# Routed attention that fetches its rows by position, another chunk order ahead of a scan, and 75 idle matmuls in place of 50

## The reference

```
h      = layernorm(x)                       # 8 x 256 x 128
logits = h @ [w_qr; w_kvr].T                # 4 query routes, 4 key routes, per token
for each route g and batch b:
    the 128 tokens with the highest query logit give queries
    the 64 tokens with the highest key logit give keys and values
    keys, values from h[those 64 tokens]; the values are scaled by sigmoid(key logit)
    8 heads of width 64, one learned null key and value in each
    out[g] = attention @ w_out, scaled by sigmoid(query logit), back to its tokens
x += mean of out over the routes that chose a token, or null_token where none did
```

## Time and profile before

| | before |
|---|---|
| median of 3 runs | 3162.34 us (3149.78 to 3163.03) |
| the profiled execution, its own time | 3159.7 us |
| its span | 3158.0 us |
| granted TensorE clock, mean | 0.952 |
| PE busy | 2790.3 us (88%) |
| PEld / DVE / ACT / POOL busy | 1829.7 / 1952.1 / 1404.1 / 1036.9 us |

### The profile page before, as it was taken

The page is one execution under the profiler, slowest core; times in us unless marked ns, Lnnn a source line. Parts: engine busy times, 40 slices in busy tenths (PEclk is TensorE's granted clock), DMA queues, the critical chain, the costliest instruction groups (busy, mean ns, idle before and its releaser), DMA issues. The chain is left out here.

```text
span 3158.0 us, 62333 instructions
## 1 busy us (share of the span) xinstructions
PE 2790.3 (88%) x24321; PEld 1829.7 (58%) x24352; DVE 1952.1 (62%) x4335; ACT 1404.1 (44%) x2960; POOL 1036.9 (33%) x1448
## 2 busy tenths in 40 slices
PE   6999799988799968887888799997999989799997
PEld 2343477756577756565556567764666556456664
DVE  7989555556555576634773566665667646466664
ACT  5655144434244435322553354443555534355553
POOL 4878223223223222312112333330222246212222
PEclk9899799999899989879999899999999999999999
DMA  2000100011000001100101000002222201112221
GB/s 79 1 1 1 54 2 1 2 25 28 1 1 2 1 1 48 66 27 20 29 22 31 15 1 1 1 4 72 67 70 70 70 18 32 59 42 73 81 67 46
DMA packets 54256, 97.07 MB, mean 31 GB/s; under 512 B 6042, under 2 KB 40870, under 8 KB 53200
## 3 DMA queue, kind: packets, MB, share of 16 engines
q1 hardware_dynamic: 52688, 92.49, 9.4%
q0 software_dynamic: 1280, 0.60, 0.1%
HBM read 71.76 MB, written 21.76 MB: 30 GB/s over the span
## 5 line engine op out<-in xcount | busy, mean ns | idle before, releaser
L566 ACT ACTIVATE s_sT<-s_R 128x1024 f32<-128x1024 f32 (+2 forms) x448 | 400.3, 946 | 199.5 <-PE s_R L500 198.6
L601 DVE TENSOR_REDUCE s_negm<-s_R 128x4 f32<-128x1024 f32 x320 | 377.2, 1221 | 153.6 <-PE s_R L471 153.5
L471 PE MATMUL s_R<-s_qk 32*128 32x256 f32 (+2 forms) x3584 | 241.8, 383 | 58.0 <-ACT s_sT L566 33.1
L500 PE MATMUL s_R<-s_qA,s_qk 32*128 32x256 f32 (+2 forms) x3584 | 240.7, 382 | 18.3 <-DVE s_negm L601 11.7
L573 ACT ACTIVATE s_oc<-s_OB 128x256 f32<-128x256 f32 x224 | 85.8, 383 | 338.3 <-PE s_OB L519 338.3
L519 PE MATMUL s_OB<-s_sT,s_v 128*32 128x256 f32 (+2 forms) x3584 | 224.1, 368 | 9.9 <-ACT s_sT L566 6.4
L471 PEld LDWEIGHTS s_R<-s_qk 32*128 32x128 f32 x3584 | 153.9, 185 | 106.1 <-issue 79.6
L616 DVE TENSOR_TENSOR s_qA<-s_qk,s_X 128x256 f32<-128x256 f32 x224 | 94.4, 421 | 194.7 <-PE s_X L531 194.7
L500 PEld LDWEIGHTS s_R<-s_qA,s_qk 32*128 32x128 f32 x3584 | 162.4, 184 | 79.2 <-issue 65.1
L1511 POOL TENSOR_TENSOR s_pr<-s_pr,s_rinv 128x1024 f32<-128x1024 f32 x64 | 121.1, 1893 | 219.6 <-DVE s_rinv L1621 219.6
L1593 ACT ACTIVATE s_pr<-s_S,s_negmax 128x256 f32<-128x256 f32 x256 | 118.5, 470 | 135.5 <-DVE s_negmax L1624 135.5
(11 more groups left out here) (585 smaller groups left out, 6307.9 us busy)
## 6 DMA issues: line engine op xcount, KB each, us to landing
s_wB<-enc_b SPq DMA_DIRECT2D x32, 962.5 KB, 4.8
s_scratch<-s_pk SPq DMA_DIRECT2D x58, 256.0 KB, 2.0
s_qk<-s_scratch SPq DMA_DIRECT2D x232, 64.0 KB
s_wA<-enc_a SPq DMA_DIRECT2D x32, 193.0 KB, 5.0
big<-moe SPq DMA_DIRECT2D x2, 2347.0 KB, 11.0
big<-routed SPq DMA_DIRECT2D x2, 2084.0 KB
all_W<-weights SPq DMA_DIRECT2D x1, 2182.0 KB, 15.5
all_W<-weights SPq DMA_DIRECT2D x1, 2181.5 KB, 10.7
```

Source lines behind the costliest of these rows:

```text
L471: last = pe.matmul(S[h][:, t * T:t * T + hi - lo], b.qk[rows, r % 2, 0, c, t * P:(t + 1) * P], b.qk[rows, r % 2, 1, c, lo:hi], start=(t == ...
L500: last = pe.matmul(b.R[:, a.turned_at(u, h // 2), :][:, h % 2, a.at(kt)], b.qk[rows, r % 2, 1, c, kt * P:(kt + 1) * P], b.qA[rows, u % 2, ...
L566: act.activation(b.sT[:, u % (a.lag + 1), 2 * p:2 * p + 2, 0:a.width], b.R[:, a.turned_at(u, p), 0:a.width], ACT.Exp).then_inc(s.expd, 1)
L601: ins = dve.tensor_reduce(b.negm[:, u % 2, :, at].rearrange("p t h -> p h t"), S.rearrange("p h (t k) -> p h t k", t=TT), AX_X, ALU.max, n ...
```

## The change

**Scan preparation.** ScalarE does `deltas(1)` and `rows(2)` ahead of `gates(3)`, and `deltas(2)` between `exp(0)` and `exp(1)`; TensorE's order follows; VectorE corrects each chunk right after its `add_one`. `keep_busy` goes from 50 matmuls to 75.

**Route stage.** SyncE also writes h to DRAM (`sent`, 1 MB). Each of the 16 rounds gets a `max_index`, which gives the positions of the eight maxima. The running count, the slots and the key mask are gone. The positions, the highest logits and the key logits are turned to have ranks on partitions (`place`, `sig`, `index`), and the count of choices comes from two matmuls on the mask.

**Main stage.** No one-hots for the gather. GpSimd fetches the rows by position with indirect DMAs, two for a unit (`fetch`: 128 rows for queries, 64 for keys), 8 units ahead. TensorE's gather is two transposes for a unit. The key scale goes into ScalarE's copy of v. The scatter's one-hot is made in its turned form at once by VectorE (`place_rows`), after the subtraction of its own unit and ahead of its sum.

```
                     rows(1)
-                    gates(3)
                     deltas(1)
                     rows(2)
+                    gates(3)
                     deltas(2)
...
-                    keep_busy(pe, g, XZ[:, 0, :], 50)
+                    keep_busy(pe, g, XZ[:, 0, :], 75)
...
                     magnitude(0)
                     magnitude(1)
+                    add_one(0)
+                    correct(0)
                     magnitude(2)
...
+                        d.done(dve.max(best[:, eight], work[:, k % 2, :]))
+                        d.mark(dve.match_replace(out=work[:, 1 - k % 2, :], in_to_replace=best[:, eight],
+                                                 in_values=work[:, k % 2, :], imm_value=NEG))
+                        d.done(dve.max_index(found[:, eight], best[:, eight], work[:, k % 2, :]))
...
+                                u = group * NB + bb
+                                at, ring = (bb % 2) * (NQ + NK), u % (2 * NB)
+                                pe.wait_ge(got_q[ring], 16 * (u // (2 * NB) + 1))
+                                pe.transpose(f[:, at:at + NQ], hq[:, ring, :], g.ident[:])
+                                pe.wait_ge(got_k[ring], 16 * (u // (2 * NB) + 1))
+                                last = pe.transpose(f[:, at + NQ:at + NQ + NK], hk[:, ring, :],
+                                                    g.ident[0:NK, 0:NK])
...
-                            for h in range(TT):
-                                pe.transpose(f[:, h * P:(h + 1) * P], sq[:, j % (2 * NB), h, :], g.ident[:])
-                            last = pe.transpose(f[0:H, 2 * P:3 * P], pn[:, j % 2, :], g.ident[:])
+                            last = pe.transpose(f[0:H, 0:P], pn[:, j % 2, :], g.ident[:])
...
+                    def fetch(u):
+                        ring = u % (2 * NB)
+                        q, k = columns(u)
+                        if u >= 2 * NB:
+                            before = u - 2 * NB
+                            pool.wait_ge(f_mm, plan.number[("gather", before // NB, before % NB // 2)] + 1)
+                        pool.indirect_dma_start(hq[:, ring, :], None, sent,
+                                                bass.IndirectOffsetOnAxis(index[:, q:q + 1], 0),
+                                                bounds_check=NTOK - 1, oob_is_err=False).then_inc(got_q[ring], 16)
...
+                    for u in range(NB):
+                        fetch(u)
+                    null_keys(0)
+                    for u in range(NB, 2 * NB):
+                        fetch(u)
...
+                        if i + 2 * NB < U:
+                            fetch(i + 2 * NB)
...
+                    def place_rows(u):
+
+                        c = columns(u)[0]
+                        if u >= 4:
+                            dve.wait_ge(scattered, u - 3)
+                        dve.tensor_scalar(sqT[:, u % 4, :], g.iota_free[:], place[:, c:c + 1], sig[:, 0, c:c + 1],
+                                          ALU.is_equal, ALU.mult).then_inc(placed, 1)
...
                                               ALU.subtract).then_inc(shifted, 1)
-                            if i % NB == 0 and i // NB + 1 < plan.GROUPS:
-                                make_onehots(i // NB + 1)
+                            place_rows(i)
                             dve.wait_ge(expd, i + 1)
```

More of the change, by code:

```diff
@@ L2650, in _ @@
                     activate(3)
+                    deltas(1)
+                    rows(2)
                     gates(3)
-                    deltas(1)
                     exp(0)
-                    rows(2)
+                    deltas(2)
                     exp(1)
-                    deltas(2)
                     rows(3)
@@ L2949, in routed_attention_stage @@
     with Stage(nc, name) as st:
-        sig = st.sb("sig", [P, TT, B, 2 * G])
-        slot = st.sb("slot", [P, TT, B, 2 * G])
+        sig = st.sb("sig", [P, 2, ROWS])
+        place = st.sb("place", [P, ROWS])
+        index = st.sb("index", [P, ROWS], mybir.dt.uint32)
+        sent = nc.dram_tensor(f"{name}_sent", (NTOK, D), F32).ap()
         rcount = st.sb("rcount", [P, TT, B])
@@ L3062, in _ @@
-                    d.done(dve.tensor_tensor(mask[:], work[:], row[:], ALU.not_equal))
-                    d.done(dve.tensor_tensor(mask_kv[:], mask_kv[:], mask[:], ALU.subtract))
-                    d.done(dve.scalar_tensor_tensor(out=mask[:], in0=mask_kv[:], scalar=g.w("r_iskv"), in1=mask[:],
-                                                    op0=ALU.mult, op1=ALU.add))
-                    d.done(dve.tensor_tensor_scan(out=csum[:], data0=ones_row[:], data1=mask[:], initial=0.0,
-                                                  op0=ALU.mult, op1=ALU.add))
@@ L3069, in _ @@
-                    d.done(dve.tensor_tensor(csum[:], csum[:], mask[:], ALU.mult))
-                    dve.tensor_scalar(csum[:], csum[:], -1.0, None, ALU.add).then_inc(slots_ready, 1)
-                    dve.wait_ge(back, 1)
-                    d.done(dve.tensor_copy(slot[:].rearrange("p h b j -> p (h b j)"), ST[:, 0:TT * ROWS]))
-                    d.done(dve.tensor_scalar(chosen[:], slot[:, :, :, 0:G], 0.0, None, ALU.is_ge))
-                    d.done(dve.tensor_reduce(count[:], chosen[:], AX_X, ALU.add))
+                        eight = slice(8 * k, 8 * k + 8)
@@ new lines, in _ @@
+                    dve.tensor_tensor(mask[:], work[:, 0, :], row[:], ALU.not_equal).then_inc(mask_ready, 1)
+                    dve.wait_ge(sig_ready, 1)
+                    d.done(dve.tensor_copy(place[:], ST[:, 0:ROWS]))
+                    d.mark(dve.tensor_tensor(index[:], place[:], g.w("r_first"), ALU.add))
+                    dve.wait_ge(counted, 1)
+                    of = LT[:, 0:TT * B].rearrange("p (h b) -> p h b", h=TT)
+                    d.done(dve.tensor_copy(count[:], of))
@@ L3268, in _, with null_keys @@
                 def _(pool):
-                    def scale_onehots(group):
+                    def null_keys(group):
                         s = plan.unit(group * NB)[0]
@@ L3507, in build_program @@
             if n == min({1, 3} & set(layers), default=None):
-                load = ("routed", P)
+                load = ("routed", T)
             if n == (8 if 8 in layers else min({9, 11} & set(layers), default=None)):
```

140 lines of the change are left out of this document (67 added, 73 removed).

## The result

The change makes the kernel slower: 3183.89 us, median of 5 runs (3183.64 to 3188.6), against 3162.34 for the kernel before. The ratio is 1.0081, with a 95% interval of 1.006 to 1.0101. The forecast was 3157.5, with a range of 3140 to 3175, and the time lies above it. The profiled execution has a span of 3181.9 us, 23.9 more than before.

The account below looks back on a forecast made before the run. TensorE was taken to bound the routed main stages' steady part. Two layers at -0.2 (main -4.6, route +4.4) and the scan's -4.3 gave -4.7: 3155 on the profiled execution, 3157.5 as median, range 3140 to 3175.

Parts of the forecast that it names:

- The new wait: Main stage: `place_rows` waits for the scatter four units back, so iterations with short front work last 6.65 us, not 5.70.
- The rival in which TensorE stays the bound: Main stage: VectorE's wait for the scatter is passed in time; a group takes 28.17, the kernel 3126 us; chance 0.15.
- the sum of the layer: One layer's main stage (-4.6) and route stage (+4.4) together: -0.2 us, twice -0.4.
- I take 1.0: Main stage: the new gather's eight transposes, at 0.11 to 0.13 each, cost TensorE 1.0 us.
- the start: Main stage: waiting for the first fetches costs 5.3 us and a slow clock about 2, together +7.3, bounds +5 and +11.
- The first group: Main stage, first four units: without the one-hots S(2) comes 7.1 after S(0), a gain of 5.4 us.
- The end of the stage: Main stage: iterations 28 to 31 lose 0.95 us each, +3.8, and iteration 32 loses +2.6.
- The route stage: `max_index` adds 0.42 us a round, 16 rounds +6.7; removed work and a shorter tail leave +4.4 a layer.
- The scan preparation: Before the scan: shorter VectorE waits give -2.9 us and a better kept clock 1.4, together -4.3.
- the rival: Scan preparation gains nothing: the wait only moves from chunk 2 to chunk 0 and the clock falls; 3162 us, chance 0.12.
- one wait of about 3.3: Scan preparation: VectorE waits once, 3.3 us from the end of magnitude(1) to the first `add_one`, in place of 6.2.
- the rival on the slow side: Main stage: VectorE and GpSimd hinder each other, each fetch call costs 2.6 us, not 1.3; 3178 us, chance 0.1.

Follow-up runs that it names:

- Run 5: The changed kernel with five buffers for the turned one-hot (`sqT`) in place of four; ratio to the kernel before 0.9996.
- run 4: The changed kernel with only the first eight units' rows fetched and reused, 16 calls a stage in place of 64; 3185.21 us in one run.
- run 12: The changed kernel with five buffers, drains, reordered transposes, 100 scan constants, and constants at main-stage starts and in the first group's gaps; 3121.12 us, ratio 0.9921.
- run 1: The kernel before with 16 more semaphores declared in each routed main stage and never used; 3160.84 us in one run beside 3155.22.
- run 7: The kernel before with only the scan preparation's part of the change: new chunk order and 75 constant matmuls in place of 50; ratio 1.0002.
- run 6: The changed kernel with 30 constant matmuls in place of 5 at each main stage's start and 20 more between the first two gathers; ratio 1.0066.
- run 3: The changed kernel with one drain instruction on GpSimd in each group of four units; ratio to the kernel before 1.0065.

## Why the prediction was wrong

The forecast for the profile was 4.7 us faster, and it is 23.9 slower, 28.6 apart. The two main stages make 17.1 of this (8.8 of it in their first groups, 4.8 in the steady parts, 2.7 at the starts, 0.8 at the ends), the two gaps behind them 9.8, the scan 2.7. The new wait, the main mechanism, was in the sum at nearly its true size. The steps that failed are a cost at the stage's end that had no term, the clock in the first group, and the price of the gather's transposes.

**The new wait was right.** `place_rows` was said to wait for the scatter and to start 0.2 after the next scores: 0.11. The iteration was put at 6.65 and is 6.60, TensorE's idle time at 1.2 and is 1.10, and GpSimd is named as the releaser. Run 5 shows that nothing else holds these iterations above TensorE's own 5.43. The rival in which TensorE stays the bound did not occur; its sum has a slip, since +7.3 - 5.4 - 21.5 - 1.6 is -21.2 and not -20.2, 2 us in its time.

**A step was missing: the gap behind the stage.** The prediction says "In steady state the fetches cost nothing", which run 4 confirms, and the sum of the layer has no term for what is settled afterwards. GpSimd's 64 calls leave 4.7 to 5.1 us a layer to the barrier, about 0.08 each, 9.8 in all. The layers of experts in the trace before gave no hint. The first issues 20 such calls, its stage ends at 1480.92 and the next begins at 1481.92. GpSimd's last call there is over at 1473.60, so that what it leaves (1.6 us by the same price, an estimate) may be settled beside VectorE's last seven microseconds; in s1a GpSimd works to 643.09, 0.6 before the end. This reading was not tested.

**The gather was too cheap.** "I take 1.0" for eight transposes; they take 1.85. The price of 0.13 was that of two like transposes in a row. With 7.27 for the gather in place of 6.65 a group is 30.18, not 29.6, and from S(4) to S(28) six groups gain 10.5 in place of 12.9. (6 x 1.57 is 9.4; the iteration behind S(4) still takes 5.42, because `place_rows` of unit 3, on which its turn depends, has no wait.)

**The start and the first group.** In s1a the start costs 9.4, not 7.3: the queries begin 13.6 us into the stage, not 12.4, and the slow clock costs 2.9 at them alone, where 2 was taken. In s3a it costs 7.9. The first group was to gain 5.4 and gains 1.3 and 0.7. In s1a S(2) comes 8.8 after S(0), not 7.1, and the iteration with the queries takes 9.34 where it takes 6.92 at full clock (run 12). The step that failed is the one that took the slow clock to be over once the front had run: it fell again at 400, after the idle gaps of the first softmax. Run 12, with these gaps filled, has the first group at 21.4, 4.6 less than before the change. The kernel before has a slow clock in its first group too (mean 0.87), and that group took 26.0 in its profile and 24.4 in run 1, so a forecast of it is no better than 1.6 us. The end of the stage was right in s1a, 6.1 against 6.4; in s3a it was 7.5, at a mean clock of 0.96.

**The route stage was right.** +4.3 in the first layer for +4.4, with 0.40 for `max_index` where 0.42 was taken. In the second it is +2.3: the logits, ahead of the search, took 7.4 us at a mean clock of 0.77 where they had taken 9.1 at 0.60. That is luck and no merit of the change, as said at the table.

**The scan preparation: nearer to the rival.** VectorE's "one wait of about 3.3" is 5.0, because ScalarE waits 1.41 and 0.64 for TensorE's `rows(2)` and `gates(3)` ahead of the first exponential, at 49.21 in place of the expected 47.9. The constants ended at 71.0, and the clock fell between 73 and 74 all the same (mean 0.56 in that slice, before 0.81). The profile has 1.6 of the 4.3, and run 7 shows no gain.

**The range.** It held the bounds of the costs that had been named. All the misses but those of the route stages and of the end of s1a went the same way, and the largest single term among them had no name; the rival on the slow side, calls of 2.6 us, did not occur. A result slower by over 0.5% had a chance of 0.1, for a reason that was not the one. GpSimd's calls took 0.94 to 1.29, the medians being 1.07 for 128 rows and 0.95 for 64. Beside VectorE's reductions and subtractions those for 128 rows took 1.06 to 1.10, with VectorE idle mostly 1.01. Timeline of both in the first group:

```profile
403.38 0.68 DVE L3354 TENSOR_REDUCE s1a_mx<-s1a_S 128x8 f32<-128x520 f32 x1
403.67 1.10 POOL L3307 DMA_INDIRECT s1a_hq<-s_sent,s_index  x1 [0.15 <-issue]
```

The rule of the Trainium skill, page "SBUF — State Buffer", section "A bandwidth-pool intuition that's wrong (but worth ruling out)", speaks of a VectorE copy, and the changed kernel's main stages have no call beside one, so they don't test it. The prediction says that the trace before has none either, which is not so for copies in general. DVE and POOL in the first layer of experts, before:

```profile
1467.41 0.29 DVE L2253 COPY s_rows<-s_TR 128x128 f32<-128x128 f32 x1 [0.71 <-PE s_TR L2123]
1467.47 0.98 POOL L2062 DMA_INDIRECT s_returned<-s_rows,s_index  x1 [2.00 <-DVE s_rows L2253]
```

The call is as long as its neighbours without a copy (0.98). Whether this copy is of the kind that the page means, no row shows.

## What to carry to other kernels

Count what a change leaves for the end of a stage as well as what it does inside: with DMAs issued by GpSimd the price there grew with their number, and a drain placed where GpSimd is idle anyway took it away. When an instruction is moved to another engine's queue, look at how old its buffer must be there: the same four buffers that were enough for a writer one iteration later held the softmax chain up when the writer came an iteration earlier, and one more buffer was worth about 27 us. And where TensorE's clock is at stake, look at every idle gap of a stretch: a filled start that ran into an unfilled first group gave only half of the expected gain (run 6).

## What the runs showed of the hardware

- Indirect DMAs of GpSimd left 0.05 to 0.08 us each to the barrier at the end of their stage (64 calls: 5.1 and 4.7 us, 16 calls: 1.2 and 0.8), even where the last was issued 250 us before. With eight drain instructions in the stage, where GpSimd had idle time, 0.45 and 0.11 us were left (run 3), and the steady part was no longer for them.
- Transposes of 128 rows and of 64 rows in alternation took 0.26 and 0.20 us each; ordered in pairs, eight took 1.29 in place of 1.85. Why the order matters was not tested.
- `max_index` on 64x256 takes 0.41, and with its load the round grows by 0.40.
- With 73 to 75 constant matmuls that ended at 71.0 the clock fell between 73 and 74; with 50 that ended at 68.8 it fell in the same slice (means of the slice 0.56 and 0.81).
